# Two cross attentions in a Perceiver kernel: a step's value groups moved ahead of its products with the values

## The reference

```python
# L0: 16 heads of 64                           # L1: 8 heads of 64
k, v = split(context @ w_kv)                   xn = layernorm(context, ln_x_g, ln_x_b)
q    = norm(x) @ w_q                           ln = layernorm(norm(x), ln_l_g, ln_l_b)
attn = softmax(q @ k.T * scale)                k, v = split(concat([xn, ln]) @ Wkv)
out  = relu((attn @ v) @ w_out1) @ w_out2      attn = softmax(where(mask, (ln@Wq*s) @ k.T*s, -max))
x    = x + layernorm(out) * gamma              x    = x + layernorm((attn @ v) @ Wo)
```

## Time and profile before

| | |
|---|---|
| median of 3 runs | 2818.84 us (2818.42 to 2819.49) |
| profiled execution | 2818.76 us, its span 2817.1 us |
| PE busy over the span | 2606.9 us (93%), mean granted clock 0.953 |
| DVE, ACT, POOL busy | 1666.4, 1389.3, 671.2 us |
| steps of `l0x` | from about 21 to 1291 us of the span |
| steps of `l1x` | from about 1467 to 2026 us |

### The profile page before, as it was taken

How to read it: one execution, slowest core, us unless ns; L and a number is a source line. 1 busy time by engine, 2 the same in 40 slices (tenths; PEclk the granted TensorE clock), 3 DMA queues, 4 the chain that set the end, 5 groups by cost and what they waited for, 6 DMA issues and landing times. The chain is left out here.

```text
span 2817.1 us, 68667 instructions
## 1 busy us (share of the span) xinstructions
PE 2606.9 (93%) x25987; PEld 2208.6 (78%) x25987; DVE 1666.4 (59%) x4284; ACT 1389.3 (49%) x2649; POOL 671.2 (24%) x888
## 2 busy tenths in 40 slices
PE   8999999999999999997859999999877478999986
PEld 6888888888888888886848888888657367888873
DVE  5667566655666566655875555555553348666625
ACT  5555555555555555552735556555410203555553
POOL 1323132312232132302025454554010100101000
PEclk9999999999999999998989999999878689999996
DMA  4011110111011110002821111111048462344310
GB/s 164 17 52 41 54 40 29 41 54 54 14 54 41 54 34 35 28 15 104 299 77 67 67 35 66 67 67 38 13 177 297 153 235 79 120 132 133 103 45 27
DMA packets 64824, 226.70 MB, mean 80 GB/s; under 512 B 12524, under 2 KB 21952, under 8 KB 59040
## 3 DMA queue, kind: packets, MB, share of 16 engines
q1 hardware_dynamic: 61840, 209.11, 21.9%
q0 software_dynamic: 2304, 8.39, 0.9%
q10 hardware_dynamic: 368, 4.92, 0.4%
HBM read 196.33 MB, written 26.05 MB: 79 GB/s over the span
## 5 line engine op out<-in xcount | busy, mean ns | idle before, releaser
L469 PE MATMUL l0x_psum<-l0x_fast 128*128 128x512 f32 x1764 | 432.9, 397 | 2.8 <-ACT l0x_sbuf L593 1.3
L469 PEld LDWEIGHTS l0x_psum<-l0x_fast 128*128 128x128 f32 x1764 | 323.4, 188 | 69.0 <-ACT l0x_sbuf L593 1.7
L604 ACT ACTIVATE l0x_sbuf<-l0x_sbuf 128x896 f32<-128x896 f32 x224 | 233.3, 1042 | 236.7 <-DVE l0x_sbuf L718 236.7
L1725 ACT ACTIVATE ahead<-l3x_psum 128x512 f32<-128x512 f32 x392 | 220.9, 598 | 200.5 <-PE l3x_psum L1666 193.5
L1793 DVE CUSTOM_DVE_ANT_0 l3x_sbuf<-l3x_psum,key_bias,l3x_sbuf 128x896 f32<-128x896 f32 x224 | 249.3, 1150 | 94.5 <-PE l3x_psum L1648 77.5
L449 PE MATMUL l0x_psum<-l0x_fast 128*128 128x448 f32 x1344 | 291.8, 366 | 1.1 <-DVE l0x_fast L704 1.1
L449 PEld LDWEIGHTS l0x_psum<-l0x_fast 128*128 128x128 f32 x1344 | 251.3, 188 | 25.9 <-DVE l0x_fast L704 1.5
L718 DVE CUSTOM_DVE_ANT_0 l0x_sbuf<-l0x_psum,l0x_sbuf 128x896 f32<-128x896 f32 x224 | 249.0, 1150 | 20.6 <-PE l0x_psum L484 20.5
L855 POOL TENSOR_TENSOR l0x_sbuf<-l0x_sbuf 128x2 f32<-128x2 f32 x112 | 31.1, 278 | 890.6 <-ACT l0x_sbuf L621 890.6
L704 DVE TENSOR_TENSOR l0x_fast<-l0x_psum,l0x_fast 128x448 fp32r<-128x448 f32 x224 | 136.2, 615 | 129.3 <-ACT l0x_fast L579 129.3
L1664 PE MATMUL l3x_psum<-l3x_fast,key_bias 128*128 128x256 f32 x784 | 209.1, 296 | 0.7 <-DVE l3x_fast L1803 0.7
(11 more groups left out here) (717 smaller groups left out, 5275.7 us busy)
## 6 DMA issues: line engine op xcount, KB each, us to landing
ahead<-in_L_ffn_W SPq DMA_DIRECT2D x32, 1024.0 KB, 4.8
last_keys<-ctx_high SPq DMA_DIRECT2D x98, 224.0 KB, 3.6
l0x_sbuf<-in_ctxT SPq DMA_DIRECT2D x14, 896.0 KB, 6.2
l0x_sbuf<-in_ctx_rows SPq DMA_DIRECT2D x14, 896.0 KB, 4.5
ctx_high<-l0x_fast SPq DMA_DIRECT2D x14, 896.0 KB, 7.8
ctx_low<-l0x_fast SPq DMA_DIRECT2D x14, 896.0 KB, 10.5
soon<-in_ctxT SPq DMA_DIRECT2D x14, 896.0 KB, 5.0
ahead<-in_ctx_pairs SPq DMA_DIRECT2D x56, 224.0 KB, 3.7
```

The lines of the kernel that those rows point to most:

```text
L469: mm = pe.matmul(ps[:, :], x[:, c, t * T:(t + 1) * T], weights[w][:, c, :], start=(j == 0), stop=(j == len(products) - 1))
L604: act.activation(self.p[:, (2 * m + a) % 4, 0:width], self.sm[:, a, 0:width], ACT.Exp, scale=-1.0, bias=self.negm[:, n % 2, 2 * pr + a:2 * ...
L1725: act.activation(p[:, u % R, :, :, :].rearrange("p h a t -> p (h a t)"), ps_t[slot["tiles", u]][:, :], ACT.Exp).then_inc(s.sem("p"), 1)
```

## The change

In PE's program the groups and the sum of a step come right behind its scores; the products with the values, the transposes and the turn come last. `uses` follows. ACT copies the first group ahead of the first exponential and the other groups between the two exponentials; both copies of transposes and `alpha` come behind the second exponential. DVE adds the side's sum in the same step, behind the maxima, and no longer at the head of the next one. The rest of DVE's order and POOL's and SP's programs stay as they are.

```diff
@@ uses
             uses += [("k", m + 1, i) for i in range(self.parts_of(m + 1))]
-            if 0 < m <= self.M:
-                uses += [("ta", m - 1, 1), ("tb", m - 1, 1)][:1 if self.short(m - 1) else 2]
             uses += self.plan.get(m, [])
             if side is not None and self.closes(m):
                 uses.append(("sum", m // P, 0))
+            if 0 < m <= self.M:
+                uses += [("ta", m - 1, 1), ("tb", m - 1, 1)][:1 if self.short(m - 1) else 2]
@@ pe
             if m < self.M:
                 self.pe_scores(pe, m)
+            if m == 0:
+                pe.wait_ge(s.sem("w_low"), 2 if self.side is None else 3)
+            for use in self.plan.get(m, []):
+                self.pe_group(pe, use)
+            if self.side is not None and self.closes(m):
+                self.side.pe_sum(pe, m // self.P, self.pe_slot(pe, "sum", m // self.P, 0))
             if m >= 2:
                 self.pe_values(pe, m - 2)
             if 0 < m <= self.M:
@@
             if m >= 2:
                 self.pe_turn(pe, m - 2)
-            if m == 0:
-                pe.wait_ge(s.sem("w_low"), 2 if self.side is None else 3)
-            for use in self.plan.get(m, []):
-                self.pe_group(pe, use)
-            if self.side is not None and self.closes(m):
-                self.side.pe_sum(pe, m // self.P, self.pe_slot(pe, "sum", m // self.P, 0))
@@ act
+            mine = self.plan.get(m, [])
+            for use in mine[:1]:
+                self.act_group(act, use)
             if m < self.M:
                 self.act_exp(act, m, 0)
-            if 0 < m <= self.M:
-                self.act_turned(act, m - 1, 1)
+            for use in mine[1:]:
+                self.act_group(act, use)
             if m < self.M:
                 self.act_exp(act, m, 1)
             if 0 < m <= self.M:
+                self.act_turned(act, m - 1, 1)
                 self.act_turned(act, m - 1, 0)
-            if 0 < m <= self.M:
                 self.act_alpha(act, m - 1)
-            for use in self.plan.get(m, []):
-                self.act_group(act, use)
@@ dve
-            if self.side is not None and m > 0 and self.closes(m - 1):
-                n = (m - 1) // self.P
-                self.side.dve_summed(dve, n, self.ps_kv[self.slot["sum", n, 0]])
             for i in range(self.parts_of(m + 1)):
                 self.dve_keys(dve, m + 1, i)
             if m < self.M:
                 self.dve_max(dve, m, 0)
                 self.dve_max(dve, m, 1)
+            if self.side is not None and self.closes(m):
+                n = m // self.P
+                self.side.dve_summed(dve, n, self.ps_kv[self.slot["sum", n, 0]])
```

## The result

The changed kernel takes 2957.8 us (median of 4 runs, 2956.9 to 2959.8); the kernel before took 2818.6 us in 4 runs beside it. The ratio is 1.0496, with a 95% interval of 1.0478 to 1.0514: slower by 139 us. The forecast was 2948 us in a range of 2895 to 3010. The profiled execution's span is 2958.1 us, against 2817.1.

The account below looks back on a forecast made before the run. PE's own program was taken to bound both stages. Terms of 29 + 26 + 2 + 22 + 29 + 19 + 2 = 129 us on 2818.76 gave 2948 us, with a range of 2895 to 3010.

Parts of the forecast that it names:

- the four waits: PE's waits before the first group: three in `l0x` (26, 22 and 29 us), one in `l1x` (19 us).
- PE's order, 161 steps: Steps with groups and products: 0.09 more for the exit to L529, 0.09 for keys behind the turn; 29 us.
- wait before the first group, `pr` 5: `l0x`: DVE's scales of `pr` 4 delay L705, so PE waits 1.89 us in 14 chunks; 26 us.
- the same, `pr` 3: `l0x`: DVE's side work of `pr` 2 delays L705, so PE waits 0.16 us in 14 chunks; 2 us.
- the same, `pr` 6 (L732 held by L1068): `l0x`: POOL's scaling at `pr` 5 holds L732, L705 comes late, PE waits 1.58 us 14 times; 22 us.
- the same, `pr` 2 (L732 held by L820): `l0x`: L732 at `pr` 1 stands behind one L820, L705 comes late, PE waits 2.26 us; 29 us.
- `l1x`, step `4n+2`: First group of the next chunk needs both L820, which now start later; PE waits 1.48 us 13 times; 19 us.
- chunk 2 over its order; all that is left: Small terms together +2 us: chunk 2's decay operations, first steps, steps without groups at the ends.
- The tie at `pr` 1: `l0x`: L820 at t + 1.20 against L732 at t + 1.22; L820 taken to win, holding L732 for one; 29 us.
- rivals 2 and 3: At `pr` 1, L732 gets ahead of L820 (2921 us, chance 0.15), or stands behind both L820 (2984 us, chance 0.15).
- rival 4: PE's clock falls behind each of the 27 waits of 1.9 us or more: 65 us more, 3013 us; chance 0.09.
- Rival 1: DVE and POOL are ready, the waits are covered and only PE's order costs, 29 us: 2848 us; chance 0.10.

Follow-up runs that it names:

- Experiment 7: Changed kernel with PE's groups and sum between products and transposes, `alpha` early, last `a=1` transposes behind `a=0`, DVE's side work behind its products' copy: 2841.3 us.
- experiment 4: Changed kernel with `alpha` early on ACT, and L732 and then DVE's side and decay work moved behind the maxima: 2943.4 us, ratio 1.0438.
- Experiments 2 and 3: Each from the changed kernel: 2 moves L732 alone behind the maxima, 2905.5 us; 3 moves ACT's `alpha` back behind the first exponential, 2904.5 us.

## Why the prediction was right, and where its terms were off

The forecast was 10 us (0.3%) low, and the causes that it named are the main ones: the order on PE and the four waits make 113 of the 141.0 us that the span is longer. That the total came so near is in part luck. Its terms for the waits were some 19 us too high together, and the order, the clock and chunk 2 with the rest some 31 too low. The account term by term, each over the order's 0.21:

| term | forecast | measured |
|---|---|---|
| PE's order, 161 steps | 29 | 161 x 0.21 = 34 |
| wait before the first group, `pr` 5 | 26 | 13 x 1.68 = 22 |
| the same, `pr` 3 | 2 | 0 |
| the same, `pr` 6 (L732 held by L1068) | 22 | 13 x 1.41 = 18 |
| the same, `pr` 2 (L732 held by L820) | 29 | 11 x 1.88 = 21 |
| half clock behind that wait | 0 | 9 x 1.58 = 14 |
| `l1x`, step `4n+2` | 19 | 13 x 1.39 = 18 |
| chunk 2 over its order; all that is left | 2 | 9.8 + 4.3 = 14 |

The 4.3 is the remainder, not a sum of its own; in it are 2.7 us between the last scores of `l0x` and the first of `l1x`, and the 1.58 won in the first step.

- **PE's order.** Right in kind and place; the exit to L529 costs 0.13, not the 0.09 taken from the sum's rows. Experiment 7 bears out both of its terms apart: with the groups elsewhere the 0.13 of the exit is gone and the 0.09 of the keys is still there. What the prediction didn't have is that an order without the fourth change costs 0.06 and not 0.21.
- **The waits.** All four stand where the prediction put them, released by L705 and, in `l1x`, by L820. Each is 0.1 to 0.4 us shorter than forecast, and 0.12 of this, at the three that L705 ends, is one number. The prediction let PE go on 0.77 us after L704's start, from the earlier trace rows; here it is 783.72 to 784.37, 0.65, and 0.64 to 0.65 at the other two. Rows 5 are of another kind of place: there transposes (L505) come behind L704, here a group (L469). The clock isn't the reason, though half clock was granted in part of that stretch. Transposes started 0.77 after L704 at a granted clock of 1.00 too (279.19 to 279.96), in the wait of the earlier trace rows, whose L704 is the first row below; and in experiment 4 a group started 0.68 after its L706 with 0.50 granted (1591.29 to 1591.97):

```profile
279.19 1.15 DVE L704 TENSOR_TENSOR l0x_fast<-l0x_psum,l0x_fast 128x448 fp32r<-128x448 f32 x2
...
1591.29 1.15 DVE L706 TENSOR_TENSOR l1x_fast<-l1x_psum,l1x_fast 128x448 fp32r<-128x448 f32 x2 [10.25 <-ACT l1x_fast L579]
...
1591.97 1.65 PE L469 MATMUL l1x_psum<-l1x_fast 128*128 128x512 f32 x3 [5.03 <-DVE l1x_fast L706]
```

The 0.12 also covers most of the 0.16 forecast for `pr` 3, which has none.

- **The tie at `pr` 1.** L820 led by 0.07, not 0.02, and L732 was held for one of the two: the case taken, with rivals 2 and 3 refused by the 2.06 us. Experiments 2 and 3 remove it from either side. The Trainium skill's page "SBUF — State Buffer", section "SBUF: two separate sides", which lets the one that starts first keep the shared ports for a whole instruction, agrees with this. The count was one too high: chunks 1 to 12, since the step at `pr` 2 of chunk 0 has no wait and chunk 13 has no next one.
- **The clock, rival 4.** It was put aside because the waits are short and stand alone, at a chance of 0.09, and a fall of the clock in these chunks was named as a sign of being wrong. It came in part: behind the 1.80 us wait in nine chunks of eleven, at 1.58 us each and not 2.4, and never in an ordinary chunk behind those of 1.61 and 1.34 us. This term, 14 us, is larger than the whole miss. The Trainium skill's page "TensorE: Matmul & The Clock Gate", section "Why this matters for your kernels", warns of long idle gaps alone; by it the clock would have stayed up here, and the measurement says otherwise. What sets chunks 3 and 12 apart from the others is open.
- **Chunk 2.** Set at about nothing, as part of 2 us; it lost 9.8 over its order, of which some 5 are the waits at `pr` 2, 5 and 6 that the forecast had counted with the other chunks, and the rest waits and falls around the decay operations.
- **Rival 1** (waits covered, 2848) is refused by the waits above. The kernel of experiment 7 has none of them in its ordinary chunks and takes 2841.

## What to carry to other kernels

When a block of an in-order engine moves ahead, work out for each releaser how late it may start and what its engine does from a common starting point up to then; here such sums gave four waits to within 0.4 us. Take such a price from the same pair of pieces as the place where it is used: from L704's start to PE's it was 0.77 us for transposes and 0.65 to 0.68 for a group in the places looked at here, and the 0.68 was at half clock. And don't add up single repairs: an operation that takes part in a tie with another engine (L732 with POOL) turns up in a new tie once something ahead of it moves, as in experiment 4.

## What was not expected of the hardware

- A small DVE operation that meets a run of POOL instructions without gaps is held to the end of the one that is running and goes in ahead of the next: 2.06 and 2.08 us behind L820, 3.14 behind L1068.
- The half clock came behind a wait of 1.80 us in chunk 7 and not behind one of 1.82 in chunk 3, with the same work before it; and in experiment 4 behind 2.54 us in chunk 5 and not in chunk 6. The length of the wait alone doesn't decide.
- The order with one more change of shape in a step costs PE 0.15 us here (10.27 against 10.12 for a two-group step of `l1x`), with the same matmuls.
